# Macaron layer on one core: attention's transposes ahead of the first context transposes, statistics at other steps

## The chip, the cores and the metric

One core of a Trainium2 chip runs the whole layer. The metric is the time of one execution in microseconds of the device (us), the median of several runs. Beside it stands one execution under the hardware profiler, from which every row below comes.

## The reference

The input is 32 sequences of 256 tokens with 128 features, in float32. Three stages follow one another, each on a layer norm of what the stage before left:

```python
x = x + 0.5 * ffn(layernorm(x), k0, k1, k2, s0, s1, s2)
x = x + attention(layernorm(x), Wq, bq, Wk, bk, Wv, bv, gamma, beta)
x = x + 0.5 * ffn(layernorm(x), k0, k1, k2, s0, s1, s2)

def ffn(x, ...):                       # weights are +1 or -1
    h = s0 * (concat([x, -x]) @ W0)    # 256 -> 512
    h = s1 * (2 * relu(h) @ W1)        # 512 -> 512
    return s2 * (2 * relu(h) @ W2)     # 512 -> 128

def attention(x, ...):                 # 16 heads of 8, sequence 256
    ctx = softmax(Q @ K.T / sqrt(8)) @ V
    return layernorm(ctx + x, gamma, beta)
```

## The kernel before

The 8192 tokens are cut into 16 tiles of 512 (two sequences each). One iteration `t` of the main schedule carries several tiles at once: the attention scores and the first half of the softmax of tile t, the second half and the context of tile t-1, the projections Q, K and V of tile t+1, a first feed-forward (`ffn_b`, of tile t+2) and a second feed-forward (`ffn_a`, of tile t-2). There are two iterations ahead of the loop (t = 0 and 1), twelve in it (t = 2 to 13) and three behind it (t = 14, 15 and 16).

An iteration has 32 steps. Every engine has its own program (`steps(it)`) and walks through these steps in order; engines meet at semaphores alone, so the order written by hand in each program is the schedule. On TensorE (PE) an even step begins with the scores of one pair of heads' lanes (`scores`, L693, into `ps_s`) and the transposed scores (`shifted`, L706, into `ps_t`). Behind them come, where the tables say so: the context products (`context`, L744, into `ps_c`), a transpose of row maxima (`max_transpose`, L769), a piece of a feed-forward (`ffn_piece`, L598 to L627, through the two banks `ps_z`) and a user of the one bank `ps_m`. These users are `CT0` and `CT1` (transposes of the context of tile t-1, L756), `LNT` (transposes of the normalized tile t+1, L658), `Q` and `K` (L667) and `V` (L678). Each waits in `misc_wait` until the user before it has been read out (`m_free`). A feed-forward is 16 pieces: piece 0 transposes its input, pieces 2 to 5 are its first product, 6 to 13 its second, 14 and 15 its third; `ffn_b` lies on steps 0 to 15, `ffn_a` on steps 16 to 31. In the iterations with a `pace` (t = 0, 14, 15, 16) there is only one feed-forward, spread out by a table.

ScalarE (ACT) and VectorE (DVE) each take one half of reading out a bank. DVE does at step s what PE did at step s-1 for the feed-forward, and at step s itself the row maxima (`row_maxima`, L1117), after which PE may write `ps_s` again. DVE also makes the statistics of the layer norms: `stats` (L1044) at one step and `mean_var` (L1050) at a later one, by the tables `AT_STATS_A` (for `ffn_a`), `AT_STATS_B` (next `ffn_b`), `AT_STATS_PREP` (attention of the tile after next) and `AT_STATS_TAIL` (the norm behind attention, halves 0 and 1 of tile t-1).

GpSimd (POOL) does the rest of the norms and splits the row maxima into two float16 parts, `max_parts` (`split_max`, L506 to L509), which PE needs for `max_transpose`. Its order in an iteration of the loop is: `split_max(t-1, 3)`, `att_norm(t+1)`, `tail_base(t)`, `ffn_norm(ffn_a)`, `split_max(t, 0)`, `tail_y` and `tail_norm` of half 0, `split_max(t, 1)`, `split_max(t, 2)`, `tail_y` of half 1, `ffn_norm(next ffn_b)`, `tail_norm` of half 1. PE's `max_transpose` of (t, 0), (t, 1), (t, 2) and (t, 3) stand at steps 10, 19, 26 and at step 3 of the next iteration (`AT_MAX`, untouched by the change).

The queue of SyncE loads tiles, stores them, spreads Q and K over rows and places the row maxima, in an order that the change doesn't touch.

Of the kernel before, what the change touches and what calls it, by code (L numbers as in the profile page):

```python
# [42 lines left out]

PIECES = 16
PACE_ZERO = {5 + piece: piece for piece in range(PIECES)}
PACE_ALONE = {8 + piece * 23 // 15: piece for piece in range(PIECES)}
PACE_LAST = {3 + piece: piece for piece in range(PIECES)}


MISC = [("CT0", 7), ("LNT", 9), ("Q", 12), ("K", 14), ("CT1", 23), ("V", 29)]  # L50
AT = dict(MISC)
AT_ZERO = {"LNT": 2, "Q": 4, "K": 6, "V": 8}
AT_OWN_LAST = {"CT0": 7, "CT1": 19}
AT_LAST = {"CT0": 3, "CT1": 9}
# [10 lines left out]
SPREADS_FIRST = 4  # L65
PROBS = 6
WARM_UP = 16
AT_STATS_A, AT_STATS_B, AT_STATS_PREP = (3, 6), (23, 27), (19, 26)
AT_STATS_A_ALONE, AT_STATS_B_ZERO, AT_STATS_PREP_ZERO = (3, 4), (28, 29), (25, 31)
AT_STATS_NEXT_A, AT_STATS_NEXT_A_LAST = 27, 15  # L70
AT_STATS_TAIL, AT_STATS_TAIL_EARLY, AT_STATS_TAIL_LAST = (11, 28), (11, 22), (8, 11)


FFN_IN = {2: 0, 3: 1, 4: 2, 5: 3}
# [6 lines left out]
class Iteration:  # L81


    def __init__(self, t, par, cur=True, prev=True, prep=True, ffn_a=None, ffn_b=None,
                 next_a=None, next_b=None, misc_base=None, pace=None, own_contexts=False):
        self.t, self.par, self.cur, self.prev, self.prep = t, par, cur, prev, prep
        self.ffn_a, self.ffn_b = ffn_a, ffn_b
        self.pace = pace
        self.next_a, self.next_b = next_a, next_b
        self.own_contexts = own_contexts  # L90
        self.stats_a = cur and ffn_a is not None
        names = [n for n, _ in MISC if
                 (n in PREP_USES and prep) or (n in ("CT0", "CT1") and prev)]
        self.misc = {n: misc_base + i for i, n in enumerate(names)}


def macaron_layer(nc, x, wq, bq, wk, bk, wv, bv, gamma, beta, k0, k1, k2, s0, s1, s2, out):
# [5 lines left out]
    with ExitStack() as ctx:  # L103
# [183 lines left out]

        def at(it, name):

            if not it.cur:  # L290
                return AT_LAST[name]
            if it.own_contexts:
                return AT_OWN_LAST[name]
            return (AT if it.prev else AT_ZERO)[name]

        def at_max(it):

# [163 lines left out]
        def _(pool):  # L461
# [30 lines left out]
            def ffn_norm(f, src):  # L492
                at_least(pool, z_full, Z_USES * f - (Z_USES - 1))
                pool.wait_ge(f_mv, f + 1)
                normalize(ffn_xn[:], src[:], ffn_mv, ffn_xc, ffn_ve, ffn_rs, TT, f_rs, 2 * f, f_xn)
# [55 lines left out]
            def steps(it):  # L551
                t, par = it.t, it.par
                if it.prev:
                    split_max(t - 1, 3)
                alone = it.pace and it.stats_a
                if alone:
                    ffn_norm(it.ffn_a, x2[par])
                if it.prep:
                    att_norm(t + 1, 1 - par)
                if not it.prev:  # L560
                    ffn_norm(it.ffn_b, x0)
                if it.cur:
                    tail_base(t, par)
                if it.stats_a and not alone:
                    ffn_norm(it.ffn_a, x2[par])
                if it.cur:
                    split_max(t, 0)
                if it.prev:
                    tail_y(t - 1, 0, 1 - par, it.misc["CT0"])
                    tail_norm(t - 1, 0, 1 - par)  # L570
                if it.cur:
                    split_max(t, 1)
                    if not it.own_contexts:
                        split_max(t, 2)
                if it.prev:
                    tail_y(t - 1, 1, 1 - par, it.misc["CT1"])
                if it.next_b is not None:
                    ffn_norm(it.next_b, x0)
                if it.prev:
                    tail_norm(t - 1, 1, 1 - par)  # L580
                if it.own_contexts:
                    split_max(t, 2)
                if it.next_a is not None:
                    ffn_norm(it.next_a, x2[1 - par])
# [5 lines left out]
        def _(pe):  # L590
# [41 lines left out]
            def ffn_piece(f, s):  # L632

                if s == 0:
                    ffn_transpose(f)
                elif s in FFN_IN:
                    ffn_in(f, FFN_IN[s])
                for at, lo, hi in FFN_MID:
                    if s == at:
                        for n in range(lo, hi):  # L640
                            ffn_mid(f, n)

                for k in FFN_OUT_AT.get(s, ()):
                    for i in range(TT):
                        ffn_out(f, i, k)
# [8 lines left out]
            def att_transpose(t, par, use):  # L654
                misc_wait(use)
                pe.wait_ge(a_xn, t + 1)
                for i in range(TT):
                    last = pe.transpose(ps_m[:, i * P:(i + 1) * P], att_xn[par][:, i, :], ident[:])  # L658
                last.then_inc(m_full, 1)
# [150 lines left out]
            def steps(it):  # L810
                t, par = it.t, it.par
                for s in range(UNITS):
                    lanes(it, s)
                    pieces = [(f, piece) for f, _, piece in ffn_work(it, s)]
                    for f, piece in pieces:
                        if piece == 0:
                            ffn_piece(f, piece)
                    tile, parity, groups = contexts(it, s)
                    for g in groups:
                        context(tile, parity, g)  # L820
                    if it.prev and s == at_max_last(it):
                        max_transpose(t - 1, 3)
                    if it.cur and s in at_max(it)[:3]:
                        max_transpose(t, at_max(it).index(s))
                    for f, piece in pieces:
                        if piece:
                            ffn_piece(f, piece)
                    if it.prev:
                        for b in range(2):
                            if s == at(it, f"CT{b}"):  # L830
                                context_transpose(t - 1, b, it.misc[f"CT{b}"])
                    if it.prep:
                        if s == at(it, "LNT"):
                            att_transpose(t + 1, 1 - par, it.misc["LNT"])
                        if s == at(it, "Q"):
                            project(0, it.misc["Q"])
                        if s == at(it, "K"):
                            project(1, it.misc["K"])
                        if s == at(it, "V"):
                            project_v(it.misc["V"])  # L840

            run(pe, steps)
            for s in range(16):
# [4 lines left out]
        def _(act):  # L848
# [47 lines left out]
            def context_copy(t, grp):  # L896
                if grp % 2:
                    act.wait_ge(c_full, 2 * GROUPS * t + grp + 1)
                    a_.activation(ctx_t[:, grp // 2, :], ps_c[:, 0:SEQ], ACT.Copy).then_inc(c_free, 1)
# [30 lines left out]
            def steps(it):  # L930
                t, par = it.t, it.par
                for s in range(UNITS):
                    if it.prev and s - 1 == at_max_last(it):
                        copy_max(t - 1, 3)
                    if it.cur and s - 1 in at_max(it)[:3]:
                        copy_max(t, at_max(it).index(s - 1))
                    tile, _, pairs = softmax_pairs(it, s)
                    for p in pairs:
                        exps(tile, p)
                    pieces = [(f, piece) for f, _, piece in ffn_work(it, s)]  # L940
                    for f, piece in pieces:
                        if piece == 0:
                            ffn_piece(f, piece)
                    tile, _, groups = contexts(it, s)
                    for g in groups:
                        context_copy(tile, g)
                    for f, piece in pieces:
                        if piece:
                            ffn_piece(f, piece)
                    if it.prep:  # L950
                        if s == at(it, "LNT"):
                            att_split(it.misc["LNT"])
                        if s == at(it, "Q"):
                            qk_split(0, it.misc["Q"])
                        if s == at(it, "K"):
                            qk_split(1, it.misc["K"])
                        if s == at(it, "V"):
                            v_copy(t + 1, 1 - par, it.misc["V"])

            run(act, steps)  # L960
            for s in range(16):
# [322 lines left out]
```

## Time and profile before

| what | value |
|---|---|
| median of 3 runs | 818.21 us (816.6 to 819.06) |
| the profiled execution, its own time | 812.72 us |
| its span in the trace | 810.8 us |
| granted TensorE clock, mean | 0.964 of full |
| PE matmul busy | 702.6 us, 87% of the span |
| DVE, ACT, POOL busy | 638.8, 514.4, 375.2 us |
| one iteration of the loop (t = 8, 403.48 to 448.09 us) | 44.61 us |

The span runs from the first to the last instruction; the execution's own time has 1.9 us around it. The profiled execution was 5.5 us shorter than the median of the three timed ones. In the loop an iteration repeats the one before it instruction by instruction, so that one of them can be read for all twelve.

### The profile page before, as it was taken

Reading aid. Unit: us, or ns where it says so; the run is one execution under the profiler, and the core shown is the slowest. Engines: PE = TensorE matmul, PEld = TensorE weight load, DVE = VectorE, ACT = ScalarE, POOL = GpSimd, SP = SyncE. Lnnn points to the kernel's source line nnn. Section 1 sums busy time; section 2 is a strip of 40 time slices with the busy share of each in tenths; the row PEclk is TensorE's granted clock in tenths of the full one; section 3 lists DMA queues with packets and bytes.
Section 4 is the critical chain, followed back from the end, with each engine's and each line's share of the span. In section 5 each row is a group of like instructions: output and inputs, shape, how many; then the busy total and the mean of one; then the engine's idle time right before and its main releaser. Section 6 shows DMA issues by size and latency. Waiting matters only on the chain.

```text
span 810.8 us, 18448 instructions
## 1 busy us (share of the span) xinstructions
PE 702.6 (87%) x7258; PEld 332.3 (41%) x7258; DVE 638.8 (79%) x1228; ACT 514.4 (63%) x739; POOL 375.2 (46%) x663
## 2 busy tenths in 40 slices
PE   6669597999999999999999999999999996977767
PEld 2334143444444444444444444444444443332332
DVE  5558588898989888888989898888889886776343
ACT  3315466677767677666777676776667775765622
POOL 4531425546372826455363727264553616254250
PEclk9989599999999999999999999999999997999897
DMA  3011001010101010110101010101101010100000
GB/s 68 19 41 47 14 3 61 15 54 10 60 16 60 15 61 16 40 35 8 57 14 61 15 60 15 61 15 41 35 8 55 14 49 15 48 15 2 15 14 13
DMA packets 29508, 25.62 MB, mean 32 GB/s; under 512 B 4336, under 2 KB 29424, under 8 KB 29424
## 3 DMA queue, kind: packets, MB, share of 16 engines
q1 hardware_dynamic: 28992, 24.07, 9.4%
q8 instruction: 58, 0.95, 0.5%
q10 hardware_dynamic: 432, 0.39, 0.1%
q14 instruction: 26, 0.21, 0.1%
HBM read 5.05 MB, written 4.19 MB: 11 GB/s over the span
## 4 chain that ended last, share of the span: by engine, by line
PE 57%; DVE 21%; ACT 9%; POOL 6%; issue 6%; DMA 0%; POOLq 0%; SPq 0%; DVEq 0%; ACTq 0%
PE ps_z L614 13%; PE ps_z L615 12%; DVE ffn_lo L1067 9%; PE ps_c L744 8%; DVE row_max L1117 6%; PE ps_s L693 6%; ACT probs L887 4%; PE ps_m L667 4%; PE ps_z L625 2%; ACT ffn_hi L854 2%; PE ps_z L598 2%; PE ps_z L627 2%; PE ps_m L678 2%; PE ps_m L756 2%; DVE ffn_bn L1044 2%
## 5 line engine op out<-in xcount | busy, mean ns | idle before, releaser
L1117 DVE TENSOR_REDUCE row_max<-ps_s 128x4 f32<-128x1024 f32 x256 | 312.1, 1219 | 66.3 <-PE ps_s L693 63.7
L887 ACT ACTIVATE probs<-ps_t,score_scale 128x1024 f32<-128x1024 f32 x256 | 284.2, 1110 | 61.5 <-PE ps_t L706 60.0
L854 ACT ACTIVATE ffn_hi<-ps_z 128x512 f16<-128x512 f32 x288 | 167.6, 591 | 144.0 <-PE ps_z L615 97.6
L1067 DVE SCALAR_TENSOR_TENSOR ffn_lo<-ps_z,ffn_hi 128x512 f16<-128x512 f32 x256 | 172.6, 683 | 44.8 <-ACT ffn_hi L854 44.7
L614 PE MATMUL ps_z<-ffn_hi,w 128*128 128x512 f16 x512 | 197.3, 385 | 10.8 <-DVE ffn_lo L1067 10.7
L615 PE MATMUL ps_z<-ffn_lo,w 128*128 128x512 f16 x512 | 195.7, 382 | 0.0
L693 PE MATMUL ps_s<-k_rows,q_rows 32*128 32x256 f16 x1024 | 102.7, 279 | 36.0 <-DVE row_max L1117 32.4
L744 PE MATMUL ps_c<-probs,v_cols 128*32 128x256 f32 x2048 | 133.5, 389 | 0.2 <-issue 0.2
L706 PE MATMUL ps_t<-q_rows,k_rows 32*128 32x256 f16 x1024 | 102.5, 279 | 3.9 <-ACT probs L887 3.8
L614 PEld LDWEIGHTS ps_z<-ffn_hi,w 128*128 128x128 f16 x512 | 50.3, 98 | 85.9 <-DVE ffn_lo L1067 24.3
L506 POOL TENSOR_TENSOR max_scaled<-row_max,max_unit 128x16 f32<-128x16 f32 x64 | 14.2, 222 | 152.2 <-DVE row_max L1117 152.2
L744 PEld LDWEIGHTS ps_c<-probs,v_cols 128*32 128x32 f32 x2048 | 57.2, 110 | 54.7 <-issue 27.9
L693 PEld LDWEIGHTS ps_s<-k_rows,q_rows 32*128 32x128 f16 x1024 | 29.2, 93 | 120.6 <-DVE row_max L1117 63.4
L625 PE MATMUL ps_z<-w,ffn_hi 128*128 128x128 f16 x512 | 64.5, 220 | 7.8 <-DVE ffn_lo L1067 7.6
L615 PEld LDWEIGHTS ps_z<-ffn_lo,w 128*128 128x128 f16 x512 | 50.5, 99 | 46.1 <-issue 1.8
L627 PE MATMUL ps_z<-w,ffn_lo 128*128 128x128 f16 x512 | 64.0, 219 | 0.0
L604 PE MATMUL ps_z<-ffn_hi,w 128*128 128x512 f16 x128 | 51.8, 404 | 6.6 <-DVE ffn_lo L1070 4.4
L625 PEld LDWEIGHTS ps_z<-w,ffn_hi 128*128 128x128 f16 x512 | 48.9, 98 | 19.2 <-DVE ffn_lo L1067 10.9
L627 PEld LDWEIGHTS ps_z<-w,ffn_lo 128*128 128x128 f16 x512 | 50.1, 98 | 1.9
L605 PE MATMUL ps_z<-ffn_lo,w 128*128 128x512 f16 x128 | 50.9, 398 | 0.0
L516 POOL TENSOR_TENSOR att_y<-ctx_n,xn_bv 128x256 f32<-128x256 f32 x32 | 23.2, 726 | 55.1 <-DVE ctx_n L1130 55.1
L485 POOL TENSOR_TENSOR tail_ve<-tail_mv,eps 128x2 f32<-128x2 f32 x32 | 6.3, 196 | 85.3 <-DVE tail_mv L1050 85.3
(122 smaller groups left out, 968.0 us busy)
## 6 DMA issues: line engine op xcount, KB each, us to landing
x<-L_attn_x SPq DMA_DIRECT2D x16, 256.0 KB, 2.7
q_rows<-q_hi SPq DMA_DIRECT2D x32, 128.0 KB, 2.4
y<-x SPq DMA_DIRECT2D x16, 256.0 KB, 2.1
k_rows<-k_hi SPq DMA_DIRECT2D x30, 128.0 KB, 2.1
q_rows<-q_lo SPq DMA_DIRECT2D x16, 128.0 KB, 2.1
q_rows<-no_max SPq DMA_DIRECT2D x16, 128.0 KB, 2.1
k_rows<-k_lo SPq DMA_DIRECT2D x15, 128.0 KB, 2.1
q_rows<-max_rows SPq DMA_DIRECT2D x64, 8.0 KB
```

Source lines behind the costliest of these rows:

```text
L604: pe.matmul(o[:], w0[:, m * P:(m + 1) * P], ffn_hi[:, 0, :], start=True, stop=False)
L614: pe.matmul(o[:], w, ffn_hi[:, 1 + k, :], start=(k == 0), stop=False)
L615: last = pe.matmul(o[:], w, ffn_lo[:, 1 + k, :], start=False, stop=(k == KC - 1))
L625: pe.matmul(o, ffn_hi[:, 5 + k, i * P:(i + 1) * P], w2[:, k, :], start=(i == 0 and k == 0), stop=False)
L627: last = pe.matmul(o, ffn_lo[:, 5 + k, i * P:(i + 1) * P], w2[:, k, :], start=False, stop=(i == TT - 1 and k == KC - 1))
L693: return pe.matmul(ps_s[:, i, a * SEQ:(a + 1) * SEQ], q_rows[par][r, g, c:c + P], k_rows[par][r, g, b * SEQ:(b + 1) * SEQ], start=True, st ...
L706: return pe.matmul(ps_t[:, i, a * SEQ:(a + 1) * SEQ], k_rows[par][r, g, c:c + P], q_rows[par][r, g, b * SEQ:(b + 1) * SEQ], start=True, st ...
L744: last = pe.matmul(ps_c[ROWS * j:ROWS * (j + 1), 0:SEQ], v[:, col:col + ROWS], probs[n % PROBS][:, j, a * SEQ:(a + 1) * SEQ], start=(a == ...
L854: a_.activation(ffn_hi[:, use, :], ps_z[use % 2][:], ACT.Relu if use else ACT.Copy, scale=1.0 if use else XN_SCALE).then_inc(z_hi, 1)
L887: a_.activation(probs[n % PROBS][:, j:j + 2, :], ps_t[:], ACT.Exp, scale=score_scale[:, 0:1]).then_inc(s_exp, 1)
L1067: v.scalar_tensor_tensor(out=ffn_lo[:, use, :], in0=ps_z[use % 2][:], scalar=0.0, in1=ffn_hi[:, use, :], op0=ALU.max, op1=ALU.subtract).th ...
L1117: v.tensor_reduce(row_max[hb % 2][:].rearrange("p (a l) e -> p l a e", a=2)[:, j:j + 2, :, g % 2], ps_s[:].rearrange("p l (a k) -> p l a k ...
```

## The change

It changes no arithmetic. It moves work between steps, and within a step.

1. In iterations of the loop and t = 1, LNT goes from step 9 to 6 and is now ahead of CT0, which goes from step 7 to 10. K goes from 14 to 15, CT1 from 23 to 22, V from 29 to 30. Iteration 14 gets a table of its own, and the pace of iterations 14 and 15 begins a step later.
2. Statistics move: A from (3, 6) to (2, 9), B from (23, 27) to (26, 27), PREP from (19, 26) to (18, 20), TAIL from (11, 28) to (18, 28); the first number is the step of `stats`, the second that of `mean_var`, except in TAIL, where the two numbers are the steps of `stats` for halves 0 and 1 and `mean_var` follows a step later. For iterations 14 and 15, A goes from (3, 4) to (2, 3).
3. On PE the users CT0, CT1, LNT and V stand ahead of the feed-forward piece of their step, no longer behind it; on ACT so do the read-outs of LNT and V. Q and K stay behind.
4. On POOL, in iterations 14 and 15 only, `split_max(t, 0)` moves ahead of `att_norm` and `tail_base`.

```diff
-PACE_ALONE = {8 + piece * 23 // 15: piece for piece in range(PIECES)}
+PACE_ALONE = {9 + piece * 22 // 15: piece for piece in range(PIECES)}
-MISC = [("CT0", 7), ("LNT", 9), ("Q", 12), ("K", 14), ("CT1", 23), ("V", 29)]
-AT = dict(MISC)
+AT = {"LNT": 6, "CT0": 10, "Q": 12, "K": 15, "CT1": 22, "V": 30}
+AT_ALONE = {"CT0": 7, "LNT": 11, "Q": 14, "K": 17, "CT1": 22, "V": 30}
-AT_STATS_A, AT_STATS_B, AT_STATS_PREP = (3, 6), (23, 27), (19, 26)
-AT_STATS_A_ALONE, AT_STATS_B_ZERO, AT_STATS_PREP_ZERO = (3, 4), (28, 29), (25, 31)
+AT_STATS_A, AT_STATS_B, AT_STATS_PREP = (2, 9), (26, 27), (18, 20)
+AT_STATS_A_ALONE, AT_STATS_B_ZERO, AT_STATS_PREP_ZERO = (2, 3), (28, 29), (25, 31)
-AT_STATS_TAIL, AT_STATS_TAIL_EARLY, AT_STATS_TAIL_LAST = (11, 28), (11, 22), (8, 11)
+AT_STATS_TAIL, AT_STATS_TAIL_EARLY, AT_STATS_TAIL_LAST = (18, 28), (11, 22), (8, 11)
...
+        self.at = (AT_LAST if not cur else AT_OWN_LAST if own_contexts else AT_ZERO if not prev
+                   else AT_ALONE if pace else AT)
...
 # POOL
                 if alone:
                     ffn_norm(it.ffn_a, x2[par])
+                    split_max(t, 0)
...
-                if it.cur:
+                if it.cur and not alone:
                     split_max(t, 0)
 # PE
-                    for f, piece in pieces:
-                        if piece:
-                            ffn_piece(f, piece)
                     if it.prev:
                         for b in range(2):
                             if s == at(it, f"CT{b}"):
...
                     if it.prep:
                         if s == at(it, "LNT"):
                             att_transpose(t + 1, 1 - par, it.misc["LNT"])
+                        if s == at(it, "V"):
+                            project_v(it.misc["V"])
+                    for f, piece in pieces:
+                        if piece:
+                            ffn_piece(f, piece)
+                    if it.prep:
                         if s == at(it, "Q"):
                             project(0, it.misc["Q"])
                         if s == at(it, "K"):
                             project(1, it.misc["K"])
-                        if s == at(it, "V"):
-                            project_v(it.misc["V"])
```

On ACT the read-outs `att_split` (LNT) and `v_copy` (V) move ahead of the pieces in the same way. `self.misc`, the count of a bank's users, is now sorted by the steps of the iteration's own table.

## Rows read from the trace of the kernel before

**Rows 1.** The page: span, then busy us, share and instructions of two engines.
```profile
span 810.8 us, 18448 instructions
PE 702.6 (87%) x7258; PEld 332.3 (41%) x7258; DVE 638.8 (79%) x1228; ACT 514.4 (63%) x739; POOL 375.2 (46%) x663
```

**Rows 2.** Iteration 8: us; busy PE, PEld, DVE, ACT, POOL; PE clock; DMA share; GB/s.
```profile
403.48:448.09 44.61, 41.92 (x454) 20.18 (x452) 39.05 (x75) 31.64 (x46) 22.77 (x41) 1.00 0.11 35
```

**Rows 3.** Waits of PE in iteration 8: total us, times, longest.
```profile
PE ps_s L693 <- DVE row_max L1117: 1.0, 2, 0.5
PE ps_m L658 <- DVE ctx_n L1130: 0.8, 1, 0.8
PE ps_z L625 <- DVE ffn_lo L1067: 0.5, 1, 0.5
PE ps_z L614 <- DVE ffn_lo L1067: 0.4, 2, 0.2
```

**Rows 4.** Timeline of POOL, iteration 8: start, duration, instruction, idle before it.
```profile
414.33 0.20 POOL L485 TENSOR_TENSOR ffn_ve<-ffn_mv,eps 128x4 f32<-128x4 f32 x1 [2.56 <-DVE ffn_mv L1050]
...
418.06 0.22 POOL L509 TENSOR_TENSOR max_parts<-max_scaled,max_parts 128x16 f16<-128x16 f32 x1
...
423.45 0.20 POOL L485 TENSOR_TENSOR tail_ve<-tail_mv,eps 128x2 f32<-128x2 f32 x1 [4.49 <-DVE tail_mv L1050]
...
427.62 0.22 POOL L509 TENSOR_TENSOR max_parts<-max_scaled,max_parts 128x16 f16<-128x16 f32 x1
```

**Rows 5.** Timeline of DVE, iteration 8.
```profile
413.82 0.37 DVE L1050 BATCH_NORM_AGGREGATE ffn_mv<-ffn_bn 128x2 f32<-128x6 f32 x4
...
416.67 0.35 DVE L1125 RECIPROCAL den<-ps_m 128x32 f32<-128x32 f32 x1
...
420.89 0.48 DVE L1044 BATCH_NORM_STATS2 tail_bn<-att_y 128x6 f32<-128x128 f32 x2
...
423.14 0.24 DVE L1050 BATCH_NORM_AGGREGATE tail_mv<-tail_bn 128x2 f32<-128x6 f32 x2
...
425.28 0.68 DVE L1067 SCALAR_TENSOR_TENSOR ffn_lo<-ps_z,ffn_hi 128x512 f16<-128x512 f32 x1
...
429.81 1.23 DVE L1117 TENSOR_REDUCE row_max<-ps_s 128x4 f32<-128x1024 f32 x1
...
432.10 0.86 DVE L1044 BATCH_NORM_STATS2 att_bn<-x 128x6 f32<-128x128 f32 x4
```

**Rows 6.** Timeline of PE, iteration 8.
```profile
413.96 0.60 PE L756 MATMUL ps_m<-ident,ctx_t 128*128 128x128 f32 x4
414.50 0.28 PE L693 MATMUL ps_s<-k_rows,q_rows 32*128 32x256 f16 x2
...
417.53 0.66 PE L658 MATMUL ps_m<-ident,att_xn 128*128 128x128 f32 x4 [0.80 <-DVE ctx_n L1130]
418.12 0.28 PE L693 MATMUL ps_s<-k_rows,q_rows 32*128 32x256 f16 x2
...
418.44 0.28 PE L769 MATMUL ps_c<-ident,max_parts 128*16 128x128 f16 x2
...
423.51 0.28 PE L693 MATMUL ps_s<-k_rows,q_rows 32*128 32x256 f16 x2
...
424.75 0.38 PE L667 MATMUL ps_m<-att_hi,wt_hi 128*128 128x512 f16 x1
...
431.15 0.28 PE L769 MATMUL ps_m<-ident,max_parts 128*16 128x128 f16 x2
```

**Rows 7.** As rows 2, around a long wait of PE in iteration 15.
```profile
744.00:747.00 3.00, 1.05 (x17) 0.40 (x16) 1.48 (x2) 1.14 (x3) 2.77 (x6) 1.00 0.00 0
747.00:750.00 3.00, 1.63 (x13) 0.59 (x14) 0.78 (x1) 1.11 (x2) 1.14 (x4) 0.79 0.02 5
750.00:753.00 3.00, 3.00 (x19) 0.99 (x21) 1.25 (x6) 0.83 (x2) 0.00 (x0) 0.64 0.01 3
```

**Rows 8.** Timeline of PE in iteration 15.
```profile
748.36 0.27 PE L769 MATMUL ps_c<-ident,max_parts 128*16 128x128 f16 x2 [3.31 <-POOL max_parts L509]
```

More of the change, by code:

```diff
@@ L91, in __init__ @@
         self.stats_a = cur and ffn_a is not None
-        names = [n for n, _ in MISC if
-                 (n in PREP_USES and prep) or (n in ("CT0", "CT1") and prev)]
-        self.misc = {n: misc_base + i for i, n in enumerate(names)}
+        self.at = (AT_LAST if not cur else AT_OWN_LAST if own_contexts else AT_ZERO if not prev
+                   else AT_ALONE if pace else AT)
+        names = [n for n in self.at if (n in PREP_USES and prep) or (n in ("CT0", "CT1") and prev)]
+        self.misc = {n: misc_base + i for i, n in enumerate(sorted(names, key=self.at.get))}
 def macaron_layer(nc, x, wq, bq, wk, bk, wv, bv, gamma, beta, k0, k1, k2, s0, s1, s2, out):
@@ L288, in at @@
         def at(it, name):
[L290 to L294, printed above, removed]
+            return it.at[name]
         def at_max(it):
@@ L946, in steps @@
                         context_copy(tile, g)
+                    if it.prep:
+                        if s == at(it, "LNT"):
+                            att_split(it.misc["LNT"])
+                        if s == at(it, "V"):
+                            v_copy(t + 1, 1 - par, it.misc["V"])
                     for f, piece in pieces:
@@ L950, in steps @@
                     if it.prep:
-                        if s == at(it, "LNT"):
-                            att_split(it.misc["LNT"])
                         if s == at(it, "Q"):
@@ L956, in steps @@
                             qk_split(1, it.misc["K"])
-                        if s == at(it, "V"):
-                            v_copy(t + 1, 1 - par, it.misc["V"])
             run(act, steps)
```

## The prediction

> **What bounds the kernel now.** I read the page first: TensorE (PE) is busy for 87% of the span, the next engine for 79% [rows 1]. Twelve of the sixteen tiles pass through the loop, so I took one iteration of it alone: 41.92 of its 44.61 us are PE's, at the full clock [rows 2]. What PE loses there, some 2.7 us, the view of waits names: two waits for DVE's row maxima (1.0 us), one of LNT for CT0's read-out (0.8), and waits for the second halves of feed-forward read-outs (0.9) [rows 3]. The loop is bound by PE's own queue, in its written order. All that a better order can win there is these 2.7 us, 12 x 2.7 = 32 us. What a worse one can lose has no such limit, because PE walks in order: whatever stands at its head and waits holds all behind it.
>
> Then I followed who must be done before each instruction that the change puts earlier or later. PE's `max_transpose` waits for POOL's `max_parts`, and POOL walks in order too: `split_max(t, 0)` stands behind `ffn_norm(ffn_a)`, which waits for the statistic A, and `split_max(t, 1)` stands behind `tail_norm` of half 0, which waits for the statistic TAIL. The timeline of POOL shows both orders [rows 4]. The change makes both statistics later and leaves `AT_MAX`, and POOL's order in the loop, alone.
>
> **First stall, step 10 of 12 iterations.** Today the mean of A starts at 413.82 [rows 5], POOL starts on it at 414.33 and `max_parts` is done at 418.06 + 0.22 = 418.28 [rows 4], 4.46 us after the mean's start. PE uses it at 418.44 [rows 6]: just in time. At step 9 the mean takes the place where CT0's reciprocal stands today, 416.67 [rows 5]. PE is ahead of the old time there by 0.16 us: LNT (0.59 us, 417.53 to 418.12) now stands before that point, CT0 (0.54 us, 413.96 to 414.50) no longer does [rows 6], and 0.2 us of a wait at step 6 go under LNT [rows 3]. So `max_parts` is ready at 416.67 - 0.16 + 4.46 = 420.97, and PE goes on at about 421.07. PE itself would arrive at 418.44 - 0.16 - 0.59 - 0.96 = 416.73 (LNT and the gap before it are gone; 0.8 us of that gap is the wait [rows 3], the rest its tail). PE stands still for 4.3 us. Against the old schedule the point is 2.6 us later and CT0's 0.54 us come behind it: +3.2 us. This holds the gain of the new order, the 0.8 us of LNT and the 0.2 us, already. Queued behind the waiting transpose are CT0, the products of steps 10 and 11 and the next scores, and for these wait ACT and DVE, so nobody else fills the gap.
>
> **Step 15.** K filled the time in which DVE makes the last hidden part, whose read-out ends at 425.28 + 0.68 = 425.96, 2.45 us after the scores of step 14 (423.51) [rows 5, 6]. Without K ahead of it PE needs 1.24 us to the place where K began (424.75) [rows 6] and about 0.4 for half a piece more: it waits 0.8 us. The cover could cost nothing if the maxima came earlier, at most K's own 0.9. I take +0.8.
>
> **Second stall, step 19 of 14 iterations (t = 1 to 14).** The mean of TAIL was made at 423.14; POOL took it at 423.45 and had `max_parts` of (t, 1) at 427.62 + 0.22 = 427.84, 4.7 us after the mean's start, 3.3 us before PE wanted it (431.15) [rows 4 to 6]. Now half 0 is summed at step 18. Behind the row maxima of that step (429.81, 1.23 us) DVE has the tail's statistics (0.48), attention's, moved to this step too (0.86), and a read-out (0.68), with starts up to 0.1 us closer than these durations say [rows 5]: the mean starts at about 432.9. POOL's same 4.7 us lead to 437.6, PE stood there at 431.15. PE stands still for 6.4 us: +6.4. The slack of 3.3 us is used up, and the mean is 9.7 us later. I see no way for these two chains to run beside each other: one is the input of the other by POOL's order.
>
> **What comes back.** LNT, CT1 and V stand ahead of pieces, A and PREP fall into gaps of DVE ahead of a read-out. Of the waits of rows 3, beside those counted, 1.7 us are left; in them I give 1.0 back (bounds 0 and 1.7). Statistics B at step 26 makes `ffn_norm` of the next tile some 0.7 us later, under the 8 us that PE has until it needs it. SyncE's spreads of Q and K start a step later and have more time than before, since the iteration is longer. All the work moved is the same work: no DMA, instruction or wait is added. One iteration: 3.2 + 0.8 + 6.4 - 1.0 = +9.4 us.
>
> **The clock.** Both stalls are longer than a wait that the trace shows: in iteration 15 PE waited 3.31 us for the same `max_parts` [rows 8]. After it the granted clock was 0.79 over 3 us and 0.64 over the next 3 [rows 7]: between the levels 2.4 and 1.2 GHz, so (0.21 + 0.36) x 3 = 1.7 us of full clock were lost. Part of a slow stretch can lie in the stall and cost nothing, so I take 1.5 us for each stall (bounds 0, if the clock stays up, and 3.4, two such stretches): +3.0 an iteration. The Trainium skill ("TensorE: Matmul & The Clock Gate", section "HAM oscillation — how this bites in real kernels") says that a gap of PE inside a loop can drop the clock to half at every pass, so that the cost is paid each time; by it the sum stays as it is, without it 3.0 us an iteration fall away. Rows 7 agree.
>
> **Outside the loop.** t = 1 has the second stall alone: 6.4 + 1.5, less 0.4 of a wait that it hides, +7.5. In t = 14 `split_max(t, 0)` no longer stands behind `att_norm` and `tail_base`. `ffn_norm`, a norm of the same size as `att_norm`, takes the 3.7 us from 414.33 to 418.06 less the two small operations of `split_max` [rows 4]; with `tail_base` that is some 5 us earlier. PE can use part of it: I take 4 back (bounds 0 and 5) against 6.4 + 1.5 of the second stall, +4. In t = 15 the same reordering gives 2 back (bounds 0 and 4). t = 0 and 16 keep their tables.
>
> **The sum.** 12 x (9.4 + 3.0) = 149, + 7.5 + 4 - 2 = 158. On the profiled execution's own time of 812.7 that is 971; the median of the timed runs is 5.5 us above it, 818.2, which gives 976. I say 973.
>
> **The rivals.**
> (a) Both stalls, and the clock stays up: 12 x 9.4 + 6 + 2.5 - 2 = 119, so 938. For it: over all of iteration 8 the clock is 1.00 in spite of small waits [rows 2]. Against it: rows 7.
> (b) Both stalls, and every fall costs two slow stretches, 3.4 us: 12 x (9.4 + 6.8) + 15 = 209, so 1024. For it: PE is less busy between stalls than today. Against it: rows 7 show it back at full clock within one.
> (c) The first stall is hidden, by DVE reaching step 9 early: then step 10 wins 1.2 us instead of losing 3.2, and with one fall of the clock an iteration costs 9.4 - 4.4 + 1.5 = 6.5: 12 x 6.5 + 9 = 87, so 905. It decides at 4.3 us earlier for the mean, more than all of DVE's work in step 8; I hold it unlikely.
> (d) Not slower: the mean of TAIL is early enough. The place is step 19; `max_parts` must be ready at 431.15, so the mean must start by 426.4 [rows 4, 6]. If it did and (c) held, PE would win most of the 2.7 us: 818 - 12 x 2 = 794. Against it: step 18's row maxima alone start at 429.81 [rows 5], after that point, and PE gives the scores for them only just before.
>
> **How the numbers follow.** The forecast has 0.75, (a) 0.09, (b) 0.07, (c) 0.06, (d) 0.02, and 0.01 is left for no change. The unknown terms move the forecast by 12 x 1 us for what comes back, by some 15 us for the clock and by 4 us for the ends: 950 to 998. For eight times in ten I reach towards (a) and (b): 938 to 1002. Slower than 0.3% (about what this kernel's measurement tells from nothing) hold all cases but (d) and the last: 0.97; faster 0.02, same 0.01.
>
> **What would show it.** An iteration of the loop of 55 to 58 us. In PE's waits, `max_transpose` for POOL's `max_parts` first by far: about 12 x 4.3 us on `ps_c` (step 10), 14 x 6.4 on `ps_m` (step 19), 140 us together. POOL's longest idle times are ahead of the first instruction of `tail_norm` and of `ffn_norm`. LNT's wait for `ctx_n` is gone. The granted clock is below 0.95 in nearly all of the forty slices. I am wrong if the iteration is under 50 us; then one of the two chains runs earlier than I placed it.

## The result and the profile after

The changed kernel takes 987.43 us (median of 4 runs, 986.41 to 988.81), the kernel before 817.4 us (4 runs). The ratio is 1.2115 (95% interval 1.2074 to 1.2156): 170 us slower. The forecast was 973, its range 938 to 1002.

The page of the kernel after, to be read beside [rows 1]: span, busy time, granted TensorE clock in forty slices of 24.6 us.

```profile
span 984.6 us, 18448 instructions
PE 763.0 (77%) x7258; PEld 343.3 (35%) x7258; DVE 644.8 (65%) x1228; ACT 511.4 (52%) x739; POOL 375.9 (38%) x663
...
PEclk9877979898998989899898989989898898789997
```

DVE, ACT and POOL do the same work in nearly the same time (644.8, 511.4 and 375.9 us busy; 638.8, 514.4 and 375.2 before). PE's share falls from 87% to 77%, so it stands still more. Its busy time rises by 60 us with the same 7258 matmuls: they run slower. The clock's row changes between 7, 8 and 9 along the whole span; the mean granted clock is 0.894, where it was 0.964.

Iteration 8 again, from scores to scores, to be read beside [rows 2]:

```profile
491.20:549.19 57.99, 46.30 (x454) 21.01 (x453) 39.56 (x75) 31.43 (x46) 22.83 (x41) 0.91 0.08 27
```

57.99 us in place of 44.61. PE's waits in this iteration (492 to 550 us), beside [rows 3]:

```profile
PE ps_m L767 <- POOL max_parts L506: 6.2, 1, 6.2
PE ps_c L767 <- POOL max_parts L506: 4.2, 1, 4.2
PE ps_z L623 <- DVE ffn_lo L1067: 0.9, 2, 0.7
PE ps_s L691 <- DVE row_max L1117: 0.2, 1, 0.2
```

The two waits at the head were not there. LNT's wait for `ctx_n` is gone, the one for row maxima nearly so. The timelines of POOL, DVE and PE in the same iteration show what is late, beside [rows 4 to 6]; one fence for each engine.

```profile
504.47 0.20 POOL L482 TENSOR_TENSOR ffn_ve<-ffn_mv,eps 128x4 f32<-128x4 f32 x1 [4.46 <-DVE ffn_mv L1050]
...
508.20 0.22 POOL L506 TENSOR_TENSOR max_parts<-max_scaled,max_parts 128x16 f16<-128x16 f32 x1
...
526.14 0.20 POOL L482 TENSOR_TENSOR tail_ve<-tail_mv,eps 128x2 f32<-128x2 f32 x1 [14.56 <-DVE tail_mv L1050]
...
530.30 0.22 POOL L506 TENSOR_TENSOR max_parts<-max_scaled,max_parts 128x16 f16<-128x16 f32 x1
```

```profile
503.96 0.37 DVE L1050 BATCH_NORM_AGGREGATE ffn_mv<-ffn_bn 128x2 f32<-128x6 f32 x4
...
522.93 1.23 DVE L1117 TENSOR_REDUCE row_max<-ps_s 128x4 f32<-128x1024 f32 x1 [0.21 <-PE ps_s L691]
524.07 0.48 DVE L1044 BATCH_NORM_STATS2 tail_bn<-att_y 128x6 f32<-128x128 f32 x2
524.46 0.85 DVE L1044 BATCH_NORM_STATS2 att_bn<-x 128x6 f32<-128x128 f32 x4
525.23 0.67 DVE L1067 SCALAR_TENSOR_TENSOR ffn_lo<-ps_z,ffn_hi 128x512 f16<-128x512 f32 x1
525.82 0.24 DVE L1050 BATCH_NORM_AGGREGATE tail_mv<-tail_bn 128x2 f32<-128x6 f32 x2
```

```profile
508.57 0.27 PE L767 MATMUL ps_c<-ident,max_parts 128*16 128x128 f16 x2 [4.22 <-POOL max_parts L506]
...
518.29 0.23 PE L623 MATMUL ps_z<-w,ffn_hi 128*128 128x128 f16 x1 [0.66 <-DVE ffn_lo L1067]
...
530.67 0.37 PE L767 MATMUL ps_m<-ident,max_parts 128*16 128x128 f16 x2 [6.24 <-POOL max_parts L506]
```

Read them across. From the mean of A (503.96) to the end of `max_parts` (508.42) it is 4.46 us, from the mean of TAIL (525.82) to its `max_parts` (530.52) 4.70 us, just what the kernel before had. POOL's work on both chains is unchanged; it begins later, and PE waits for its end. Ahead of `tail_ve` POOL itself was idle for 14.56 us while `split_max(t, 1)`, whose last row maxima DVE had read by 517.6, stood behind it: ready for the last 8.5 us of that time.

The granted clock around the first stall, by stretches as in [rows 7]:

```profile
506.00:508.00 2.00, 0.00 (x0) 0.00 (x0) 0.20 (x1) 0.00 (x0) 1.92 (x4) 1.00 0.00 0
508.00:510.00 2.00, 1.43 (x7) 1.08 (x8) 0.11 (x1) 0.37 (x1) 0.34 (x2) 0.71 0.00 0
510.00:512.00 2.00, 2.00 (x6) 0.73 (x5) 0.67 (x2) 0.00 (x0) 0.72 (x1) 0.50 0.02 4
512.00:514.00 2.00, 2.00 (x16) 0.68 (x15) 0.80 (x1) 1.13 (x2) 0.00 (x0) 0.94 0.00 0
```

PE does nothing between 504.3 and 508.6 us, and just as it goes on the clock is at its lower level (0.50 is 1.2 of 2.4 GHz) for some 3.4 us (the rows fall short of 1.00 by 0.29, 0.50 and 0.06 over 2 us each; at half speed that is 2 x 2 x 0.85 = 3.4). None of it lies in the stall. The same view around the second stall:

```profile
528.00:530.00 2.00, 0.00 (x0) 0.00 (x0) 0.00 (x0) 0.00 (x0) 1.84 (x4) 0.83 0.00 0
...
536.00:538.00 2.00, 2.00 (x18) 1.09 (x18) 1.78 (x3) 1.62 (x3) 0.00 (x0) 0.96 0.19 66
```

It is 0.50 in all three stretches between these two, from 530 to 536. PE resumed at 530.67, so some 5.5 us of its work ran at half speed.

Where the 173.8 us between the two spans came from can be read off POOL's `att_ve`, which comes once in an iteration. It stands at 139.53 (t = 2) and 629.10 (t = 13) before, at 146.73 and 784.27 after. Up to t = 2: +7.2 us. Eleven iterations: 637.54 - 489.57 = +148.0, 13.45 each. From t = 13 to the end: 200.3 - 181.7 = +18.6, of which 13.4 are the iteration itself, so +5.2 for t = 14 to 16.

### The profile page after: what moved, and what is told of

It reads as the page before. It is cut to its first block, busy times and chain, and to the rows that moved or that the text cites. A ratio compares the mean times of both kernels' runs of the same rounds, so it can differ in the third digit from the quotient of the medians.

```text
span 984.6 us, 18448 instructions
## 1 busy us (share of the span) xinstructions
PE 763.0 (77%) x7258; PEld 343.3 (35%) x7258; DVE 644.8 (65%) x1228; ACT 511.4 (52%) x739; POOL 375.9 (38%) x663
## 4 chain that ended last, share of the span: by engine, by line
PE 48%; DVE 25%; POOL 14%; issue 7%; ACT 6%; DMA 0%; POOLq 0%; SPq 0%; DVEq 0%; ACTq 0%
PE ps_c L742 10%; DVE row_max L1117 9%; PE ps_z L612 7%; DVE ffn_lo L1067 7%; PE ps_z L613 7%; PE ps_s L691 5%; PE ps_m L665 3%; PE ps_z L602 3%; PE ps_z L603 3%; PE ps_m L754 2%; PE ps_z L596 2%; ACT probs L886 2%; POOL ffn_xn L487 2%; POOL ffn_xc L483 2%; POOL ffn_rs L485 2%
## 5 line engine op out<-in xcount | busy, mean ns | idle before, releaser
L612 PE MATMUL ps_z<-ffn_hi,w 128*128 128x512 f16 x512 | 207.6, 405 | 3.6 <-DVE ffn_lo L1067 3.6
L613 PE MATMUL ps_z<-ffn_lo,w 128*128 128x512 f16 x512 | 205.4, 401 | 0.0
L742 PE MATMUL ps_c<-probs,v_cols 128*32 128x256 f32 x2048 | 145.4, 416 | 0.4 <-issue 0.4
L691 PE MATMUL ps_s<-k_rows,q_rows 32*128 32x256 f16 x1024 | 107.0, 289 | 28.8 <-DVE row_max L1117 24.9
L704 PE MATMUL ps_t<-q_rows,k_rows 32*128 32x256 f16 x1024 | 106.5, 288 | 4.8 <-ACT probs L886 4.8
L742 PEld LDWEIGHTS ps_c<-probs,v_cols 128*32 128x32 f32 x2048 | 59.7, 116 | 61.5 <-issue 37.4
L612 PEld LDWEIGHTS ps_z<-ffn_hi,w 128*128 128x128 f16 x512 | 52.8, 103 | 77.2 <-issue 27.2
L767 PE MATMUL ps_m<-ident,max_parts 128*16 128x128 f16 x64 | 10.1, 249 | 88.0 <-POOL max_parts L506 88.0
L623 PE MATMUL ps_z<-w,ffn_hi 128*128 128x128 f16 x512 | 64.4, 220 | 13.4 <-DVE ffn_lo L1067 13.2
L613 PEld LDWEIGHTS ps_z<-ffn_lo,w 128*128 128x128 f16 x512 | 52.9, 103 | 53.1 <-issue 11.9
L602 PE MATMUL ps_z<-ffn_hi,w 128*128 128x512 f16 x128 | 60.6, 473 | 7.8 <-DVE ffn_lo L1070 5.3
L603 PE MATMUL ps_z<-ffn_lo,w 128*128 128x512 f16 x128 | 60.7, 475 | 0.0
L482 POOL TENSOR_TENSOR ffn_ve<-ffn_mv,eps 128x4 f32<-128x4 f32 x32 | 6.5, 203 | 132.9 <-DVE ffn_mv L1050 126.0
L623 PEld LDWEIGHTS ps_z<-w,ffn_hi 128*128 128x128 f16 x512 | 48.9, 98 | 22.5 <-DVE ffn_lo L1067 18.6
```

The source lines that it names most:

```text
L602: pe.matmul(o[:], w0[:, m * P:(m + 1) * P], ffn_hi[:, 0, :], start=True, stop=False)
L603: pe.matmul(o[:], w0[:, m * P:(m + 1) * P], ffn_lo[:, 0, :], start=False, stop=True).then_inc(z_full, 1)
L612: pe.matmul(o[:], w, ffn_hi[:, 1 + k, :], start=(k == 0), stop=False)
L613: last = pe.matmul(o[:], w, ffn_lo[:, 1 + k, :], start=False, stop=(k == KC - 1))
L623: pe.matmul(o, ffn_hi[:, 5 + k, i * P:(i + 1) * P], w2[:, k, :], start=(i == 0 and k == 0), stop=False)
L691: return pe.matmul(ps_s[:, i, a * SEQ:(a + 1) * SEQ], q_rows[par][r, g, c:c + P], k_rows[par][r, g, b * SEQ:(b + 1) * SEQ], start=True, st ...
```

## The experiments

Rival to my theory, in all of them: that the moved bank users or the late norms themselves make the loss, and not POOL's order behind two late statistics. Times are medians; ratios are to the kernel before on the same chip.

**1. Both statistics back** (3 rounds).

```diff
-AT_STATS_A, AT_STATS_B, AT_STATS_PREP = (2, 9), (26, 27), (18, 20)
+AT_STATS_A, AT_STATS_B, AT_STATS_PREP = (3, 6), (26, 27), (18, 20)
-AT_STATS_TAIL, AT_STATS_TAIL_EARLY, AT_STATS_TAIL_LAST = (18, 28), (11, 22), (8, 11)
+AT_STATS_TAIL, AT_STATS_TAIL_EARLY, AT_STATS_TAIL_LAST = (11, 28), (11, 22), (8, 11)
```

> The changed kernel with two numbers put back: A at steps (3, 6) and TAIL at (11, 28), everything else as changed. My theory (two POOL chains behind late statistics make both stalls): both waits of PE for max_parts at steps 10 and 19 are gone but for some 1 us at step 10, the clock stays up, an iteration of the loop is 44.6 to 45.5 us and the time 812 to 826 us, about that of the kernel before. Rival (the moved bank users CT0, LNT, K and V make the stalls): the time stays at 970 to 990 us.

822.36 us, ratio 1.0092 (1.0057 to 1.0127). Two numbers hold 165 of the 170 us. What stays is 0.9% slower than before; an iteration is 45.46 us. The waits of one such iteration say why, first PE's, then DVE's:

```profile
PE ps_c L767 <- POOL max_parts L506: 1.6, 1, 1.6
PE ps_z L623 <- DVE ffn_lo L1067: 0.9, 2, 0.7
PE ps_s L691 <- DVE row_max L1117: 0.8, 2, 0.5
```

```profile
DVE tail_bn L1044 <- POOL att_y L513: 0.9, 1, 0.9
```

With LNT ahead of CT0, PE is at step 10 earlier than before, and `max_parts` isn't. And with CT0 at step 10 the context's norm is made at DVE's step 11, so TAIL at 11 waits for `att_y`. So the old statistics don't fit the new places exactly. That A would have to be earlier still is my reading of these waits; no run tries it.

**2 and 3. One of them back** (1 round each): A at (3, 6), or TAIL at (11, 28), the rest as changed.

> The changed kernel with A alone back at (3, 6). Theory: the stall at step 10 falls from 4.2 us to some 1.4 us (PE arrives 1.7 us earlier than in the kernel before, so not to nothing) and the first slow stretch of the clock goes, the stall of 6.2 us at step 19 stays: iteration 53 to 54 us, time 930 to 940 us. Rival (the stalls are one delay, which the other chain takes over): time over 965 us.

> The changed kernel with TAIL alone back at (11, 28). Theory: the stall of 6.2 us at step 19 goes in 14 iterations and with it the longer slow stretch of the clock (some 2.4 us), the stall of 4.2 us at step 10 stays: iteration 49 to 50 us, time 865 to 880 us. Rival (one delay that the other chain takes over): time over 940 us.

A back: 937.51 us (ratio 1.150); the iterations from t = 2 on take 53.0 to 56.0 us, 53.8 in the mean. TAIL back: 878.27 us (1.077), iterations of 48.6 to 50.7 us, 50.0 in the mean, at the upper edge of what I expected. PE's waits over the whole span, A back first, TAIL back second:

```profile
PE ps_m L767 <- POOL max_parts L506: 88.0, 16, 6.2
...
PE ps_c L767 <- POOL max_parts L506: 23.6, 13, 4.1
```

```profile
PE ps_c L767 <- POOL max_parts L506: 55.0, 13, 4.4
```

Each stall goes alone and leaves the other whole (the changed kernel has 88.0 and 55.0). What A back leaves at step 10 is 1.6 us an iteration, (23.6 - 4.1) / 12, as in experiment 1. Undoing A wins 50 us, undoing TAIL 109, both 165: near enough the sum that the two are two losses, not one delay seen twice.

**4. POOL's order turned, every statistic as late as in the change** (3 rounds).

```diff
+                if it.cur and not alone:
+                    split_max(t, 0)
                 if it.stats_a and not alone:
                     ffn_norm(it.ffn_a, x2[par])
-                if it.cur and not alone:
-                    split_max(t, 0)
+                splits_first = it.cur and not it.own_contexts
                 if it.prev:
                     tail_y(t - 1, 0, 1 - par, it.misc["CT0"])
+                    if splits_first:
+                        split_max(t, 1)
                     tail_norm(t - 1, 0, 1 - par)
                 if it.cur:
-                    split_max(t, 1)
+                    if not (splits_first and it.prev):
+                        split_max(t, 1)
```

> The changed kernel with every statistic as late as changed, but POOL's order in iterations 1 to 14 turned: split_max(t, 0) ahead of ffn_norm(ffn_a), and split_max(t, 1) ahead of tail_norm of half 0. Theory (it is the order of POOL's queue that turns late statistics into stalls of PE): no wait for max_parts in the loop, clock up, iteration 43.2 to 44.2 us, time 795 to 812 us, so faster than both kernels. Rival (late statistics cost by themselves, through the norms that they feed or through DVE): time over 850 us.

802.21 us, ratio 0.9833 (0.9794 to 0.9872): faster than both kernels, with both statistics still late. The timeline of POOL in an iteration of 43.72 us:

```profile
411.07 0.22 POOL L506 TENSOR_TENSOR max_parts<-max_scaled,max_parts 128x16 f16<-128x16 f32 x1
413.36 0.21 POOL L482 TENSOR_TENSOR ffn_ve<-ffn_mv,eps 128x4 f32<-128x4 f32 x1 [2.06 <-DVE ffn_mv L1054]
...
421.11 0.22 POOL L506 TENSOR_TENSOR max_parts<-max_scaled,max_parts 128x16 f16<-128x16 f32 x1
429.05 0.20 POOL L482 TENSOR_TENSOR tail_ve<-tail_mv,eps 128x2 f32<-128x2 f32 x1 [7.71 <-DVE tail_mv L1054]
```

`max_parts` is there nearly 8 us before `tail_ve` begins. POOL idles for the late mean, and PE doesn't wait: its waits in this iteration are 1.6 us, none of them for `max_parts`. This is the experiment that separates the theories: the late statistics make no stall of their own, standing behind them does. Whether earlier statistics would win something more in this order, no run shows.

**5. The same turned order in the kernel before** (3 rounds), nothing else changed.

> The kernel before with POOL's order alone turned (the splits of row maxima ahead of ffn_norm(ffn_a) and of tail_norm of half 0). Theory: nothing waits for max_parts in the loop of the kernel before, so it gives nothing there: iteration 44.5 to 44.7 us, time within 4 us of the kernel before. Rival (the turned order is a gain of its own, apart from the change's new placement): 808 us or less.

816.19 us, ratio 1.0001 (0.998 to 1.0023). The order gives nothing where the statistics are early. So experiment 4's gain of some 14 us over the kernel before comes from the rest of the change: 10.7 us from the loop, 12 x (44.61 - 43.72), and the parts for t = 14 and 15, which are 2.7 us by themselves in experiment 9. What in the loop wins it (the new places of LNT, CT0, CT1 and V, the order within a step, or the statistics B and PREP) isn't separated; in the view of waits the largest part is LNT's wait of 0.8 us for `ctx_n`, which is gone, as forecast.

**6. The late statistics in the kernel before** (1 round): A at (2, 9), TAIL at (18, 28), nothing else changed.

> The kernel before with two numbers changed: A at (2, 9) and TAIL at (18, 28); all bank users, B and PREP as before. Theory (the two late statistics make the whole loss): stalls of 2.7 to 3.5 us at step 10 (PE arrives later than in the changed kernel) and 6.2 to 6.5 at step 19, iteration 56 to 58.5 us, time 970 to 1000 us. Rival (it takes the moved users too): time under 940 us.

992.96 us, ratio 1.2151. The two numbers make the whole loss without any moved bank user; an iteration is 58.0 us. Its two stalls are 3.49 and 5.69 us (I had expected 2.7 to 3.5 and 6.2 to 6.5), 1.3 us less in all than in the changed kernel, but PE's other waits are 2.6 us in place of 1.1.

**7. Work put into the stalls** (1 round). In iterations 2 to 13, right before the waiting `max_transpose`, after waits that make its bank free:

```diff
+            def fill(o, n):
+                for i in range(n):
+                    pe.matmul(o[:], ident16[:], ident16[:].unsqueeze(1).broadcast_to([P, TT, P]), start=True, stop=True)
...
                 at_least(pe, mt_free, 4 * t + hb)
+                fill(o, filler)                 # 18 at step 10, 28 at step 19
                 pe.wait_ge(s_mparts, 4 * t + hb + 1)
```

> The changed kernel, and in the twelve iterations of the loop PE makes 18 more 512-column matmuls (3.9 us) into the free bank right before it waits at step 10, and 28 (6.0 us) before it waits at step 19, with results that nobody reads: added work, inside stalls of 4.2 and 6.2 us. Theory (a slow clock after each stall costs some 1.6 and 2.4 us an iteration): the granted clock stays at 1.00 in the loop, iteration 53.8 to 54.6 us, time 935 to 952 us, so more work takes less time. Rival (the slow clock is beside the critical path, or another cause makes the 4 us): time 982 us or more.

942.57 us, 45 us less than the changed kernel with 552 more matmuls. One iteration, and the added matmuls in its timeline:

```profile
473.00:527.13 54.13, 52.42 (x506) 24.24 (x498) 39.32 (x76) 31.18 (x46) 22.83 (x42) 1.00 0.09 29
```

```profile
483.48 4.06 PE L759 MATMUL ps_c<-ident 128*128 128x512 f16 x18
487.68 0.28 PE L772 MATMUL ps_c<-ident,max_parts 128*16 128x128 f16 x2
...
501.79 6.22 PE L759 MATMUL ps_m<-ident 128*128 128x512 f16 x28
508.01 0.28 PE L772 MATMUL ps_m<-ident,max_parts 128*16 128x128 f16 x2
```

The granted clock is 1.00 and the iteration 54.13 us in place of 57.99: the slow clock cost 3.9 us an iteration, and keeping PE busy avoids it. The stalls themselves are as long as before, only filled. Half speed over 3.4 + 5.5 us of work would cost some 4.4 us. The rest is about the 0.4 us by which PE's waits for row maxima are shorter in the changed kernel (0.2 us) than here (0.6).

**8. Turned order, and K back at step 14** (3 rounds).

```diff
-AT = {"LNT": 6, "CT0": 10, "Q": 12, "K": 15, "CT1": 22, "V": 30}
+AT = {"LNT": 6, "CT0": 10, "Q": 12, "K": 14, "CT1": 22, "V": 30}
```

> The changed kernel with POOL's turned order (as in x4_splits_first) and K back at step 14. Theory (K at 15 uncovers the read-out that the third product needs): the wait of 0.66 us at step 15 is gone, iteration 43.0 to 43.2 us, time 6 to 10 us below the 802 us of x4_splits_first, 792 to 796. Rival (K at 14 makes another wait, for the bank or for ACT): within 2 us of x4_splits_first.

790.76 us, ratio 0.9674 (0.9647 to 0.9701): the fastest of all, 3.3% under the kernel before, and 11.5 us under experiment 4, somewhat more than the 6 to 10 expected. An iteration is 42.89 us. Its waits of PE are 0.9 us in all:

```profile
PE ps_s L695 <- DVE row_max L1121: 0.7, 2, 0.4
PE ps_z L627 <- DVE ffn_lo L1071: 0.2, 1, 0.2
```

**9. The parts for iterations 14 and 15 alone, in the kernel before** (5 rounds): the later pace, the table of iteration 14, A at (2, 3), `split_max(t, 0)` ahead.

> The kernel before with the change's parts for iterations 14 and 15 alone: the pace a step later, the own table for iteration 14, A at (2, 3), and split_max(t, 0) ahead of att_norm and tail_base. Loop, t = 1 and the order within a step as before. Theory (as in the prediction's last terms, without the second stall): some 4 us less in iteration 14 and 2 in iteration 15, time 5 to 8 us below the kernel before. Rival (the time saved there is lost again to the slow clock or to the later pace): within 2 us of the kernel before.

814.24 us, ratio 0.997 (0.9949 to 0.999). A gain of some 2.7 us, half of what I expected. The waits of PE that the new order of POOL can take away are those for `split_max(14, 0)` and `split_max(15, 0)`; in the kernel before they are

```profile
687.33 0.37 PE L769 MATMUL ps_c<-ident,max_parts 128*16 128x128 f16 x2 [1.47 <-POOL max_parts L509]
...
726.50 0.27 PE L769 MATMUL ps_c<-ident,max_parts 128*16 128x128 f16 x2 [1.16 <-POOL max_parts L509]
```

That is 2.6 us, and both are gone. Over the span PE's waits for `max_parts` fall from 9.0 us in six to 4.8 in two, but those for row maxima grow from 32.4 to 37.6 us. The longest of the six was never in reach: it is the one of [rows 8], for `split_max(15, 2)`, which stands behind `tail_norm` of half 1. It was 3.31 us and is now

```profile
752.24 0.37 PE L771 MATMUL ps_c<-ident,max_parts 128*16 128x128 f16 x2 [4.12 <-POOL max_parts L510]
```

## Why the prediction was right, step by step

The mechanism was right in both places, and the forecast's terms can be held against rows one by one (us an iteration of the loop):

| term | forecast | measured |
|---|---|---|
| stall at step 10 | 4.3 | 4.22 |
| wait at step 15 | 0.8 | 0.66 |
| stall at step 19 | 6.4 | 6.24 |
| iteration without the clock, against before | +9.4 | +9.5 (54.13 - 44.61, experiment 7) |
| clock | 3.0 | 3.9 (57.99 - 54.13) |
| iteration | +12.4 | +13.4 |
| ahead of t = 2 | +7.5 | +7.2 |
| t = 14 to 16 | +2 | +5.2 |

- **First stall.** Right, with its 4.46 us from mean to `max_parts`. Experiments 2, 4 and 6 show it to be A's step and POOL's order.
- **Second stall.** Right; experiments 3, 4 and 6. The prediction held these two chains to be inescapable "by POOL's order", and that order is what experiment 4 turned: with it the change as planned is a gain.
- **Step 15.** Right in kind: experiment 8 took it away. It was worth 0.83 us an iteration (43.72 - 42.89): PE's waits fall by 0.7 (1.6 to 0.9) and its busy time by 0.16 (42.03 to 41.87); why the latter, no run shows.
- **What comes back.** At full clock, in experiment 7's iteration, PE's waits are 1.5 us beside the filled stalls, 0.66 of them at step 15. So some 0.8 of the 1.7 are left and 0.9 came back, for 1.0 forecast. In the changed kernel itself only 0.4 are left, with PE slower in part of it.
- **The clock.** The step was right and its term too small, 3.0 for 3.9. I had taken each fall at what the one after a 3.31 us wait cost, 1.7 us, less a part hidden in the stall. Nothing was hidden in the first stall: the clock fell as PE resumed. After the second about 5.5 us of work ran slow, so that fall alone cost some 2.7.
- **The ends.** The 6 us given back in t = 14 and 15 were 2.7 (experiment 9). I had sized them by how much earlier POOL would be, some 5 us; PE can gain no more than it had waited there, 1.47 and 1.16 us, and the sum left these waits out. With 2.7 and the second stall of t = 14 as forecast (6.4 + 1.5) the sum would have been +5.2, as measured. That it fits to a tenth is partly luck: the stall was 6.06 us there.
- **The sum.** By the spans the loss is 173.8 us and the sum of 158 is nearly 16 short: 12.6 in the loop (12 x 1.05, nearly all of it the clock) and 3.2 at the end, less 0.3 ahead of t = 2. By the medians the loss is 170 us. Between 973 and 987 stand 14 us, because 973 was taken between two starting points, 812.7 and 818.2.

Of the rivals, (a) is refuted by the clock's rows and experiment 7, (c) and (d) by the stalls in the trace, and (b) overstated the clock.

The Trainium skill ("TensorE: Matmul & The Clock Gate", section "HAM oscillation — how this bites in real kernels") describes a loop in which a gap at every pass drops the clock at every pass. The trace agrees: two falls in each iteration, 3.9 us of its 58. [rows 7], which the prediction set beside that section, had shown one fall behind one wait outside the loop, and no fall at every pass.

## What to carry to other kernels

When an operation is made later on one engine, follow its result to the engine that reads it, and look at what stands behind the reader there: here two late means made no stall by themselves, and cost 165 us through two tiny splits queued behind them. Put the operation that another engine waits for ahead of one whose input is late, and measure a new order together with that: the change was 21% slower with one order of POOL's queue and 1.7% faster with the other. Count more than its length for a long stall on TensorE: behind stalls of 4.2 and 6.2 us work ran at half clock, for 3.9 us more. And a producer that becomes earlier is worth at most what its reader had waited for it: look that wait up first.

## What the runs showed of the hardware

Added matmuls made a kernel faster: 46 in each of twelve iterations took 45 us off, because the granted clock stayed at 1.00 (experiment 7).

The slow stretch after a stall doesn't follow from the stall's length. In the changed kernel stalls of 4.22 and 6.24 us left 3.4 and 5.5 us of work at the lower clock. In one iteration of experiment 6 it was the other way round: PE resumed at 508.20 after 3.49 us and the clock was back at about 512.9, 4.7 us later; it resumed at 528.91 after 5.69 us and the clock was back at about 533.4, 4.4 us later. Nor does the fall wait for PE to resume there: the granted clock was 0.51 from 506 to 508, while PE stood still. So a term such as my 1.5 us a stall is a mean of unlike cases.
